# Narrow attention scores issued on 64 rows, with the keys kept in two masked copies

## What is computed

```python
x = ln(x + mamba(x))                  # 512 channels, 16 states, scan over 256 steps
x = ln(x + latent_attention(x, ctx, idx))   # 16 heads of 16, each query has 64 chosen keys
x = ln(x + bitlinear_ffn(x))
x = ln(x + self_attention(x))         # 16 heads of 16, head_mask on q, k and v
x = ln(x + cross_attention(x, ctx))   # 16 heads of 64
x = ln(x + moe_ffn(x))                # 8 experts, top 6, and a shared one
# both narrow attentions, per head h:
s = q[h] @ k[h].T * 0.25              # 256 x 256, contraction over 16
out[h] = softmax(s) @ v[h]            # the latent one weighs each key by how often idx names it
```

## Time and profile before

| | |
|---|---|
| median of 3 runs | 4188.95 us (4187.92 to 4199.23) |
| the profiled execution's own time | 4191.22 us |
| its span, first to last instruction | 4189.4 us |
| mean granted clock | 0.850 |
| TensorE busy | 3465.2 us |
| VectorE busy | 3010.9 us |
| ScalarE busy | 1908.3 us |
| GpSimd busy | 649.4 us |

### The profile page before, as it was taken

How to read it: one execution, slowest core, us unless ns; L and a number is a source line. 1 busy time by engine, 2 the same in 40 slices (tenths; PEclk the granted TensorE clock), 3 DMA queues, 4 the chain that set the end, 5 groups by cost and what they waited for, 6 DMA issues and landing times.

```text
span 4189.4 us, 57527 instructions
## 1 busy us (share of the span) xinstructions
PE 3465.2 (83%) x21250; PEld 2275.8 (54%) x21250; DVE 3010.9 (72%) x6490; ACT 1908.3 (46%) x4400; POOL 649.4 (16%) x516
## 2 busy tenths in 40 slices
PE   2568888898888888888888888889888888988887
PEld 1345645556565555655555564555655555564555
DVE  5677686867878687786868768686886868778622
ACT  2235445453544445444454544545454444544413
POOL 1203030210303012030210303021030301203000
PEclk8568979798887989979898897989989798997978
DMA  6425171533616144261623517152351614426010
GB/s 217 108 71 149 45 201 44 167 96 104 171 44 181 64 137 126 72 174 43 185 85 119 149 46 199 44 171 92 116 160 44 186 59 144 119 83 187 22 43 32
DMA packets 205689, 470.84 MB, mean 112 GB/s; under 512 B 23712, under 2 KB 43808, under 8 KB 190688
## 3 DMA queue, kind: packets, MB, share of 16 engines
q1 hardware_dynamic: 205408, 467.17, 37.1%
HBM read 446.11 MB, written 20.97 MB: 111 GB/s over the span
## 4 chain that ended last, share of the span: by engine, by line
PE 52%; DVE 29%; ACT 9%; issue 7%; DMA 2%; POOL 1%; SPq 0%; DVEq 0%; ACTq 0%
PE ps L632 8%; DVE region_x L1440 4%; PE ps L809 4%; PE ps L613 3%; PE ps L924 3%; PE ps L644 3%; PE ps L560 3%; PE ps L778 3%; PE ps L823 3%; PE ps L764 2%; DVE rmax L1582 2%; PE ps L863 2%; DVE nm L1477 2%; PE ps L729 2%; PE ps L790 2%
## 5 line engine op out<-in xcount | busy, mean ns | idle before, releaser
L1223 POOL TENSOR_TENSOR region_x<-region_x 128x512 f32<-128x512 f32 x512 | 649.2, 1269 | 3205.7 <-DVE region_x L1440 3205.7
L1440 DVE TENSOR_TENSOR_SCAN region_x<-ps,region_x 128x512 f32<-128x512 f32 x512 | 622.2, 1218 | 60.3 <-ACT ps L1027 59.7
L1027 ACT ACTIVATE ps<-region_x,aneg 128x255 f32<-128x255 f32 x1024 | 440.6, 470 | 454.7 <-DVE region_x L1440 400.9
L1423 DVE TENSOR_TENSOR region_x<-region_x,ps 128x512 f32<-128x512 f32 x512 | 342.3, 670 | 49.8 <-PE ps L560 23.4
L863 PE MATMUL ps<-xTy,wide 128*128 128x256 f32 x1280 | 338.9, 420 | 21.3 <-DVE region_y L1641 21.3
L1490 DVE SCALAR_TENSOR_TENSOR region_x<-region_x,cntk 128x512 f32<-128x512 f32 x256 | 167.0, 689 | 215.3 <-ACT region_x L1063 215.3
L632 PE MATMUL ps<-region_y 32*128 32x256 f32 x1024 | 254.3, 643 | 78.1 <-ACT region_y L1063 55.5
L863 PEld LDWEIGHTS ps<-xTy,wide 128*128 128x128 f32 x1280 | 258.5, 209 | 74.4 <-DVE region_y L1641 29.4
L1144 ACT ACTIVATE region_y<-ps,rmax 128x256 f32<-128x256 f32 x512 | 235.2, 480 | 84.1 <-DVE rmax L1582 84.1
L560 PE MATMUL ps<-region_x,sely 128*32 128x512 f32 x1024 | 194.1, 841 | 89.5 <-POOL region_x L1223 89.5
L632 PEld LDWEIGHTS ps<-region_y 32*128 32x128 f32 x1024 | 145.5, 307 | 211.3 <-ACT region_y L1063 164.1
(11 more groups left out here) (243 smaller groups left out, 6669.7 us busy)
## 6 DMA issues: line engine op xcount, KB each, us to landing
region_x<-rows_of_dt SPq DMA_DIRECT2D x1024, 256.0 KB, 4.7
wide<-in_wgate SPq DMA_DIRECT2D x16, 1280.0 KB, 8.0
wide<-in_wup SPq DMA_DIRECT2D x16, 1280.0 KB, 10.6
down<-in_wmoe SPq DMA_DIRECT2D x16, 1280.0 KB, 5.5
wide<-in_wq SPq DMA_DIRECT2D x16, 1024.0 KB, 4.8
wide<-in_wk SPq DMA_DIRECT2D x16, 1024.0 KB, 7.1
wide<-in_wv SPq DMA_DIRECT2D x16, 1024.0 KB, 10.0
down<-in_wo SPq DMA_DIRECT2D x16, 1024.0 KB, 8.0
```

Of the source, the lines that this page charges most:

```text
L1027: last = f(ps[:, 1 + 2 * (k % 2), m * T + 1:(m + 1) * T], dt_rep[k % SLOTS][:, m, 1:T], ACT.Exp, scale=aneg[:, k, m:m + 1])
L1223: nc.gpsimd.tensor_tensor(hbuf[k % HSLOTS], hbuf[k % HSLOTS], csb.unsqueeze(1).to_broadcast([P, 2, T]), ALU.mult).then_inc(hc_ready, 1)
L1423: tt_(hbuf[k % HSLOTS], dtx_rep[k % SLOTS], ps[:, 2, 0:T].unsqueeze(1).to_broadcast([P, 2, T]), ALU.mult).then_inc(dbx, 1)
L1440: nc.vector.tensor_tensor_scan(flat(hbuf[k % HSLOTS]), ps[:, 1 + 2 * (k % 2), :], flat(hbuf[k % HSLOTS]), 0.0, ALU.mult, ALU.add).then_inc ...
```

## The change

The keys are written twice. The first copy has the rows of the heads with even g and zeros in the others, the second the rows with odd g. This is done by scale and bias of ScalarE's evacuation: `pick` is a new constant with two columns, one for the rows of the even and one for those of the odd heads. A matmul of the scores then takes 64 rows, 0 to 63 or 64 to 127, of the queries with the same rows of one copy; the zeros take the other head's rows out of the sum. A pair of heads is now g = u % 2 and g = u % 2 + 2, so the places of the maxima and the order of heads in `PT` follow. Four evacuations more are issued in each attention (eight instead of four), one constant more is loaded, and six small operations are added to the setup. The number of matmuls, the banks, the waits and `ORDER` are as before.

```diff
-    ("aug", (P, 4), F32), ("qb1", (P, 4), F32), ("kb1", (P, 4), F32), ("hm1", (P, 4), F32),
+    ("aug", (P, 4), F32), ("pick", (P, 2), F32), ("qb1", (P, 4), F32), ("kb1", (P, 4), F32), ("hm1", (P, 4), F32),
...
-FIRST = 20
+FIRST = 21
+        kbp, hmp, augp = sb("kbp", (P, 2, 4)), sb("hmp", (P, 2, 4)), sb("augp", (P, 2, 4))
...
-                    self.QT, self.KT = place(0, (4, T)), place(1024, (4, T))
+                    self.QT, self.KT = place(0, (4, T)), (place(1024, (4, T)), place(other_keys, (4, T)))
...
-        att0 = Attention("lat", 0, True, 0, VP0, nm0, in_x)
-        att1 = Attention("self", 4, False, 1, VP1, nm1, in_y)
+        att0 = Attention("lat", 0, True, 0, VP0, nm0, in_x, 10508)
+        att1 = Attention("self", 4, False, 1, VP1, nm1, in_y, 7424)
...
-                            r = slice(64 * (u % 2) + 32 * j, 64 * (u % 2) + 32 * j + 32)
-                            last = mm(ps[:, b + j, qt * T:(qt + 1) * T], a.QT[r, t, qt * P:(qt + 1) * P], a.KT[r, t, :],
+                            r = slice(64 * j, 64 * j + 64)
+                            last = mm(ps[:, b + j, qt * T:(qt + 1) * T], a.QT[r, t, qt * P:(qt + 1) * P], a.KT[u % 2][r, t, :],
...
-                    t, g = n // 4, n % 4
+                    t, e = n // 4, n % 4 // 2
...
-                            r = slice(32 * (g + j), 32 * (g + j) + 32)
-                            last = mm(ps[:, a.sT_bank(n + j), kt * T:(kt + 1) * T], a.KT[r, t, kt * P:(kt + 1) * P],
+                            r = slice(64 * j, 64 * j + 64)
+                            last = mm(ps[:, a.sT_bank(n + j), kt * T:(kt + 1) * T], a.KT[e][r, t, kt * P:(kt + 1) * P],
                                       a.QT[r, t, :], start=True, stop=True)
...
-                            n, h = 4 * t + g, 4 * g + t
+                            n, h = 4 * t + 2 * (g % 2) + g // 2, 4 * g + t
...
-                    last = f(att0.KT[:, t, :], bank(b)[:, t % 2, :], ACT.Identity, bias=W["aug"][:, t:t + 1])
+                    for e in range(2):
+                        last = f(att0.KT[e][:, t, :], bank(b)[:, t % 2, :], ACT.Identity, bias=augp[:, e, t:t + 1],
+                                 scale=W["pick"][:, e:e + 1])
...
-                    last = f(att1.KT[:, t, :], bank(6 + t // 2)[:, t % 2, :], ACT.Identity,
-                             bias=kba[:, t:t + 1], scale=W["hm1"][:, t:t + 1])
+                    for e in range(2):
+                        last = f(att1.KT[e][:, t, :], bank(6 + t // 2)[:, t % 2, :], ACT.Identity,
+                                 bias=kbp[:, e, t:t + 1], scale=hmp[:, e, t:t + 1])
...
+            for e in range(2):
+                for dst, src in ((kbp, kba), (hmp, W["hm1"]), (augp, W["aug"])):
+                    ts(dst[:, e, :], src[:], W["pick"][:, e:e + 1], None, ALU.mult).then_inc(setup_v, 1)
...
-                                col = 64 * (u % 2) + 32 * j + 16 + t
+                                col = 64 * j + 32 * (u % 2) + 16 + t
...
-                        last = nc.vector.tensor_reduce(at_nm[:, 2 * (u % 2):2 * (u % 2) + 2, :, 16 + t],
+                        last = nc.vector.tensor_reduce(at_nm[:, u % 2::2, :, 16 + t],
```

More of the change, by code:

```diff
@@ L270, in build, with __init__ @@
         class Attention:
-            def __init__(self, tag, base, masked=False, first_pair=0, VP=None, NM=None, place=None):
+            def __init__(self, tag, base, masked=False, first_pair=0, VP=None, NM=None, place=None, other_keys=0):
                 self.base, self.masked, self.first_pair = base, masked, first_pair
@@ L1259, in _ @@
             tt_(kba[:], kba[:], W["aug"][:], ALU.add).then_inc(setup_v, 1)
+            v.wait_ge(setup_v, n + 4)
+            for e in range(2):
+                for dst, src in ((kbp, kba), (hmp, W["hm1"]), (augp, W["aug"])):
+                    ts(dst[:, e, :], src[:], W["pick"][:, e:e + 1], None, ALU.mult).then_inc(setup_v, 1)
+            n += 6
             for buf, value in ((VP0, 1.0), (VP1, 1.0), (nm0, 0.0), (nm1, 0.0), (shiftb, 0.0), (wsplit, 0.0)):
@@ L1722, in layouts @@
     bf = np.dtype(mybir.dt.np(BF16))
+    pick = np.zeros((P, 2), np.float32)
+    for e in range(2):
+        for lower in (0, 64):
+            pick[lower + 32 * e:lower + 32 * e + 32, e] = 1
     aug, selx = np.zeros((P, 4), np.float32), np.zeros((P, 8, P), np.float32)
@@ L1749, in layouts @@
         "half": np.repeat(np.float32([0, 16]), SEL).reshape(P, 1), "ones": np.ones((P, P), np.float32), "tri": tri,
-        "aug": aug, "selx": selx.astype(bf), "sely": sely,
+        "aug": aug, "pick": pick, "selx": selx.astype(bf), "sely": sely,
         "wq0": tiles(heads16(n["L0_xattn_W_q"].T)), "wdown0": tiles(n["L0_xattn_W_kv_down"].T),
```

## The result

| | before | after |
|---|---|---|
| median | 4188.43 us (4185.15 to 4199.23, 4 runs) | 4130.76 us (4129.78 to 4132.02, 4 runs) |
| ratio to before | | 0.9858 [0.984, 0.9876] |
| the profiled execution's span | 4189.4 us | 4128.0 us |
| mean granted clock | 0.850 | 0.908 |

The kernel is 58 us faster by the medians, 61.4 by the spans; the forecast was 21. The page of the changed kernel answers to the earlier trace rows: TensorE is busy 168 us less with the same 21250 instructions, and ScalarE has its 128 instructions more. In the clock's row eight sevens have become two, and eighteen nines twenty-four.

A forecast was written before the change was run, and what follows sets the result against it. Self attention's second pass was taken as bound by TensorE at its low clock. Self attentions -37, latent ones +17, lone ones -2 and start +1 gave -21 us: 4168 us by the median, range 4118 to 4212.

The forecast's parts named there:

- the comparison of the two lone stretches: Last sequence, y stream alone: self second pass, 32-row, 86% busy, stayed at 0.50; cross attention's, 64-row, rose to 1.00.
- the latent term: Fifteen latent attentions beside cross attention: copies cost 1.64 us, 0.5 comes back, 15 x (1.64 - 0.5) = +17 us.
- So by itself the form gives nothing: Score records: two 64-row units in succession take 2.00 us at the high level, one 32-row unit 1.13; no gain without clock.
- A gain may come back between the latent passes ... I take half of it, 0.5: Between latent passes the clock drops briefly; gain bounded by 0 and 1.0 us a sequence, 0.5 taken.
- gains of about 3 each: First latent and last self attention, running alone: costs 2.3 + 1.9, gains about 3 each with the clock's rise, -2 us.
- the cap that VectorE's holes set: End of self attention's second pass: VectorE's holes of 5.3 us cap the 5.4 us a faster TensorE could save.
- Record mean under 500 ns: Sign: mean score record in self attention's second pass falls from 643 to under 500 ns.
- VectorE's holes for L1028 and L561, from 5.3 to about 1: Sign: VectorE's waits in the second pass's last 14 us, on ScalarE and TensorE, shrink from 5.3 to about 1 us.
- The first passes as long as now: Sign: first passes, measured from their first unit, keep their length.
- I am wrong if ... the latent copy of x costs nothing: Stated refutation: latent evacuations delay the copy of the transposed x, put at 1.64 us on the path.
- The first one: Rival, 15%: clock stays up through both self attention passes, -60 us, 4129 us.
- The second and the third: Rivals: evacuations and lost pairs eat the gain, 4220 or 4205 us, 15%; clock does not rise, 4266 us, 15%.

The follow-up runs named there:

- copies_only: Changed kernel with both key copies still written in both attentions, but all scores on 32 rows as before; 4250.73 us, 1.0125 of before.
- first_only: Changed kernel with both key copies, but 64-row scores only in the first passes, second passes on 32 rows; 4210.83 us, 1.0039 of before.
- self_only: Changed kernel with latent attention put back as before (one key copy, 32 rows), self attention on 64 rows; 4169.22 us, 0.9935 of before.
- no_mask: Changed kernel with the masking constant `pick` set to ones, so each score sums two heads, same instructions; 4130.7 us, 0.9838 of before.
- deferred: Changed kernel, but GpSimd makes the masked copies in both attentions and self attention's first pass takes unmasked keys on 32 rows; 4072.82 us, 0.9708 of before.

## Why the prediction was right in its direction and a third of the size

The sum by the forecast's own terms, against the stretches above:

| term | forecast | measured |
|---|---|---|
| self attention, 14 sequences | 14 x (1.93 - 4.4) = -35 | 14 x (2.30 - 1.50 + 1.03 - 3.46) = -23 |
| latent attention, 14 sequences | 14 x (1.64 - 0.5) = +16 | 14 x (1.33 - 0.81 - 0.43 - 1.20) = -15.5 |
| the rest of them | 0 | -2.5 |
| first and last sequence, start | -2 | -20.6 |
| sum | -21 | -61.4 |

**Right.** The clock decides, it rises with the rows of the records, and the comparison of the two lone stretches was a sound ground: copies_only and first_only hold the second pass at 0.50 with 32 rows, 86% busy; 64 rows bring 0.76 with TensorE busy only 17.05 of 21.10 us. The price of the copies was near too. 15 x (1.93 + 1.64) + 4.2 + 1 is 59 us by the forecast, and copies_only measured 52. Self attention gained 3.9 us in a sequence (1.50 - 1.03 + 3.46), where 4.4 stood, and its copies cost 2.3, not 1.93. These two misses go against the change, 12 us in 14 sequences. The Trainium skill, "TensorE: Matmul & The Clock Gate", section "The HAM clock gate", has the gate set by how busy the engine has been; the lone passes don't fit that, since the busier one is the slower, and nor do self_only's latent windows, busy 99% at 0.77.

**The step that failed** is the latent term, "So by itself the form gives nothing" and with it "A gain may come back between the latent passes ... I take half of it, 0.5". 2.44 us came back in a sequence, five times that, and in three places. The gap gave its 0.43. The first pass gave 0.81, as the clock no longer falls in it: it takes 14.67 us at 1.00, and 32-row ones that stood at 0.99 or more all through (in copies_only and self_only) took 14.6, so there the form by itself gives nothing, as forecast. But behind each of those the clock fell, and the gap took 6.4 us in place of 5.1; with 64 rows, in the changed kernel, the high level held through both. And 1.20 came in the second pass, which was already at 1.00, where the forecast saw nothing to win. It had compared units of one form with each other; the cost lies at the border of two forms, and the latent scores meet 64-row scores of cross attention eight times in a pass. first_only shows just under 0.2 us for each such border. The trace of before held it, in the same pass: from L812 at 2158.74 us to the 32-row unit 0.20 us, and the unit 1.06 until the next group. The Trainium skill, "TensorEngine Tiling (Array Packing)", section "Key Properties", says that changing the tiling mode drains TensorE. The trace agrees in that a change costs time, just under 0.2 us for each of the eight; that it is a drain, no run shows. This term was off by 32 us (with the copy cheaper by 0.3).

**The second miss** is the size of the lone passes: "gains of about 3 each", but each second pass went from 28.0 to 21 us. No scan runs beside them, so the cap that VectorE's holes set in the middle sequences doesn't apply: in the last self attention TensorE's busy time fell from 23.97 to 17.05 us, and the pass with it. Their first passes gave 2.7 and 2.2 us, for which nothing stood. With the copies' cost, 3.9 and 1.9 us, the two lone attentions are at -13.2 us, where -2 was forecast; the other stretches of the ends make up the rest of the -20.6.

**The marks named.** Second-pass clock 0.75 or more: 0.78, right. Record mean under 500 ns: 546, missed, since about half of the second pass is still low. L1115 and L1042 at 128 instructions: right. TensorE's wait for L1115 up by 1.9 us a sequence: from 5.6 to 33.8 us in the run, 1.8 each, right. VectorE's holes for L1028 and L561, from 5.3 to about 1: to 0.34, 1.38 and 0.17, 1.9 us, more than the 1 named. "The first passes as long as now": wrong. TensorE ends the self attention's 1.50 us sooner, but 1.03 of it returns as a longer gap, where the transposition waits for VectorE's reductions. "I am wrong if ... the latent copy of x costs nothing": it cost 1.33, and 1.43 less when GpSimd took the copies.

**The rivals.** The first one's time, 4129 us, is the one measured, but not its mechanism: it wanted the clock up through both passes of the self attention, and they are high for 0.55 and 0.51 of their length. The missing time was in the latent attention and the ends. The second and the third are excluded: self attention gained 3.9 us in a sequence in the changed kernel and the kernel with it alone is 0.65% faster, and the clock rose.

**Open.** The halves, by attention, by pass and of the repairs, don't add up to the whole, and nothing here says what makes the 32-row latent pass stand at one level or the other, or why the self attention's second pass rises where it does. I did not try to move the rise.

## What to carry to other kernels

Look at matmuls by how many rows they fill and not only by how long they keep TensorE busy: where the granted clock stays low in a busy stretch, filling the array with zeros can be worth more than the copies cost. Count the borders between record forms where two streams share TensorE, and give both the same form where they interleave. A price that lies on a full engine's path should be offered to an idle one, with the latest point at which its result is needed; here that doubled the gain (1.42% to 2.92%).

## What the runs showed of the hardware

- The granted clock followed the rows of the records and not their content: the same pass, with 128 records in each, took 28.0 us at 0.50 with 32 rows, 21.1 at 0.76 with 64 rows half of which meet zeros, and 21.0 at 0.76 with 64 rows of which none is masked (no_mask). Beside other work this did not hold alone, as the next line shows.
- A stretch of the same 232 records took 24.6 us at 1.00 or 31.3 at 0.77 within one execution, with TensorE 98% and 99% busy.
- Where records of 64 and of 32 rows stand behind one another at the higher level, eight such borders cost 1.4 us in a pass. A unit of eight records took 1.06 us when the form changed on both of its sides, with 32 rows and with 64 alike, and 0.96 to 0.97 when it changed on one or none.
- GpSimd multiplied 128x1024 fp32 by one value for each partition in 1.89 us and 128x512 by a 128x256 operand taken twice in 1.27. VectorE's scans were no slower beside it: in deferred the 15 that ran beside a mask took 1215 ns, as did the 167 beside which GpSimd did nothing.
